# Message net: edge weight in nine contraction rows and 64 columns, scatter one-hots shared between VectorE and ScalarE

## What is computed

```python
src, dst = (edge_index[0], edge_index[1])
ew = edge_weights[:, None]
n = x.shape[0]
for l in range(edge_W.shape[0]):
    m = jnp.concatenate([x[src], x[dst], ew], axis=-1)
    m = jax.nn.relu(m @ edge_W[l] + edge_b[l])
    agg = jax.ops.segment_sum(m, dst, num_segments=n)
    x = jax.nn.relu(jnp.concatenate([x, agg], axis=-1) @ node_W[l] + node_b[l])
return x
```

## Time and profile before

| | us |
|---|---|
| median of three runs | 13607.72 |
| lowest and highest | 13596.84, 13614.53 |
| the profiled execution | 13518.01 |
| its span, first to last instruction | 13516.2 |

### The profile page before, as it was taken

The page is one execution under the profiler, slowest core; times in us unless marked ns, Lnnn a source line. Parts: engine busy times, 40 slices in busy tenths (PEclk is TensorE's granted clock), DMA queues, the critical chain, the costliest instruction groups (busy, mean ns, idle before and its releaser), DMA issues. The chain is left out here.

```text
span 13516.2 us, 456920 instructions
## 1 busy us (share of the span) xinstructions
PE 11116.6 (82%) x106911; PEld 9874.1 (73%) x106912; DVE 10913.7 (81%) x40164; ACT 5219.0 (39%) x19100; POOL 2412.2 (18%) x7659
## 2 busy tenths in 40 slices
PE   3555499899898699976664879999998779999998
PEld 3444388788787599965453339999997338999998
DVE  6555499688687388876564999999997999999998
ACT  1000122222222122235452328875453237875454
POOL 2777100000000000001110001112221001222222
PEclk9999999899898599989896999999998999999999
DMA  1111377344243011123231554432221554432222
GB/s 54 53 53 50 95 236 235 104 122 121 79 123 92 10 40 40 40 55 81 67 83 49 148 138 116 115 93 73 70 73 48 140 144 114 115 99 73 70 73 61
DMA packets 1206834, 1232.86 MB, mean 91 GB/s; under 512 B 218351, under 2 KB 1042800, under 8 KB 1206106
## 3 DMA queue, kind: packets, MB, share of 16 engines
q1 hardware_dynamic: 1180954, 1228.47, 32.9%
q0 software_dynamic: 25792, 3.35, 0.2%
HBM read 1115.06 MB, written 116.16 MB: 91 GB/s over the span
## 5 line engine op out<-in xcount | busy, mean ns | idle before, releaser
L993 DVE TENSOR_SCALAR hot<-iota_row,place 128x128 f32<-128x128 f16 (+1 forms) x9000 | 1816.7, 268 | 172.8 <-PE acc L1092 149.3
L1711 ACT ACTIVATE msgs<-G,share 128x64 f32<-128x64 f32 x6000 | 1390.0, 314 | 1351.1 <-PE G L1725 1351.1
L985 DVE TENSOR_SCALAR hotT<-idx,iota_col 128x512 bf16<-128x512 f16 x4500 | 1321.7, 351 | 603.4 <-PE G L1138 562.9
L1725 PE MATMUL G<-u_b,hotT 128*128 x12000 | 1591.7, 276 | 50.3 <-DVE hotT L1659 50.3
L1735 PE MATMUL S<-msgs,hot 128*128 128x128 f32 x12000 | 1586.3, 275 | 0.0
L1157 ACT CAST msgs<-G 128x384 bf16<-128x384 f32 x2250 | 1023.2, 479 | 1447.0 <-PE G L1138 1441.1
L1725 PEld LDWEIGHTS G<-u_b,hotT 128*128 128x128 f32 x12000 | 1467.0, 193 | 51.1 <-issue 51.1
L1735 PEld LDWEIGHTS S<-msgs,hot 128*128 128x128 f32 x12000 | 1462.3, 192 | 0.0
L1080 PE MATMUL G<-table_m,hotT 128*128 x9000 | 1311.0, 248 | 150.7 <-issue 137.6
L1110 ACT ACTIVATE msgs<-sums 128x128 f32<-128x128 f32 x2250 | 699.4, 311 | 1824.2 <-DVE sums L1102 1544.0
L1547 ACT ACTIVATE msgs<-G,msgs 128x64 f32<-128x64 f32 x6000 | 1310.8, 332 | 30.7 <-issue 21.1
(11 more groups left out here) (323 smaller groups left out, 19843.4 us busy)
## 6 DMA issues: line engine op xcount, KB each, us to landing
idx<-pos_rows SPq DMA_DIRECT2D x6375, 128.0 KB, 2.9
hotT<-hots_d SPq DMA_DIRECT2D x750, 256.0 KB
hots_d<-hotT SPq DMA_DIRECT2D x375, 256.0 KB, 3.4
key_b<-key_rows SPq DMA_DIRECT2D x62, 416.0 KB
ty_b<-type_rows SPq DMA_DIRECT2D x62, 416.0 KB
rows<-rel_rows SPq DMA_DIRECT2D x1500, 6.0 KB
ew_now<-ew_rows_d SPq DMA_DIRECT2D x1125, 3.0 KB
sorted_d<-recs,place POOLq DMA_INDIRECT x806
```

Source lines behind the costliest of these rows:

```text
L985: op = eng.tensor_scalar(hotT[:, c % deep, n], idx[:, c, r], p.col[:, first:first + 1], None, ALU.is_equal)
L993: op = eng.tensor_scalar(hot[:, c % 2, q], p.row16[:], place[:, c % 2, q:q + 1], None, ALU.is_equal)
L1711: op = eng.activation(msgs[:, c % 2, 2 + j // HEADS, j % HEADS * D:(j % HEADS + 1) * D], G[c % 2][1][:, j * D:(j + 1) * D], ACT.Copy, scal ...
L1725: mm = eng.matmul(G[c % 2][b][:, k * W:(k + 1) * W], hotT[:, c % 2, q * P:(q + 1) * P], table[:, ds(dst_at(at, q, 24 * W), W)], start=True ...
```

## The change

The edge weight's product is laid out in the other direction. `ew_rows` gets nine rows (the three parts, three times over), `ew_now` nine partitions, and `we9` holds in its nine rows each part of the weight row three times: row n is part n // 3. One matmul of 64 columns with nine contraction rows gives the sum of all nine products, and it is added to the first 64 of the chunk's 192 columns.

VectorE makes two of the four scatter one-hots (`shared_hots=2`), ScalarE the other two: first Square of (position - column) into a new tile `apart`, for the next quarter (L1114), and then Relu of 1 - `apart` into `hot` (L1126), for the present one. ScalarE signals itself (`squared`) between the two. GpSimd's copy of the places waits for `made[0]` beside the wait it had.

```diff
@@ load_sorted, SyncE
-                for i in range(EW):
-                    to = s.ew_rows[i]
+                for k in range(EW * EW):
+                    to, i = s.ew_rows[k], k % EW
@@ edge_pass, SyncE
-                        eng.dma_start(extra[0][0:EW, c], extra[1][:, ds(t * (4 * P), 4 * P)]).then_inc(idx_in[c].h, 16)
+                        eng.dma_start(extra[0][0:EW * EW, c], extra[1][:, ds(t * (4 * P), 4 * P)]).then_inc(idx_in[c].h, 16)
@@ edge_pass, GpSimd
                     ready(eng, hots, t)
+                    if shared_hots < 4:
+                        ready(eng, made[0], t)
                     eng.tensor_copy(place[:, c % 2].unsqueeze(2), s.e[:, ds(t * 4, 4), 1:2]).then_inc(placed.h, 1)
@@ edge_pass, VectorE
-                    for q in range(4):
+                    for q in range(shared_hots):
                         op = eng.tensor_scalar(hot[:, c % 2, q], p.row16[:], place[:, c % 2, q:q + 1], None,
                                                ALU.is_equal)
@@ gnn_layer, gather
-                mm = eng.matmul(env["G"][h][:, k * 3 * D:(k + 1) * 3 * D], s.ew_now[:, c, q * P:(q + 1) * P],
-                                s.we3[:, l].rearrange("p q f -> p (q f)"), start=False, stop=True)
+                mm = eng.matmul(env["G"][h][:, k * 3 * D:k * 3 * D + D], s.ew_now[:, c, q * P:(q + 1) * P],
+                                s.we9[:, l], start=False, stop=True)
@@ gnn_layer, ScalarE
+        def squares(eng, t, c, env):
+            env["reach"](eng, env["placed"], t + 1)
+            env["reach"](eng, env["made"][0], t)
+            for i in range(2):
+                op = eng.activation(apart[:, c % 2, i], p.row16[:], ACT.Square, bias=env["place"][:, c % 2, 2 + i:3 + i],
+                                    scale=-1.0)
+            op.then_inc(squared.h, 1)
+
         def scalar(eng, t, c, env):
+            if isinstance(t, int) and t == 0:
+                squares(eng, 0, 0, env)
+            if not (isinstance(t, int) and t == QUARTERS - 1):
+                squares(eng, t + 1, (c + 1) % 4, env)
+            env["reach"](eng, squared, t + 1)
+            env["reach"](eng, env["scattered"][1], t - 1)
+            for i in range(2):
+                eng.activation(env["hot"][:, c % 2, 2 + i], apart[:, c % 2, i], ACT.Relu, bias=p.ones[:, 0:1], scale=-1.0)
@@ message_net
-        fetch(p, [(s.we3[i:i + 1], we_parts[:]) for i in range(3)])
+        fetch(p, [(s.we9[n:n + 1], we_parts[:, :, n // EW]) for n in range(EW * EW)])
```

More of the change, by code:

```diff
@@ L672, in _ @@
                                   ew_rows[0:n, i, full, :]).then_inc(ld.h, 16)
-                ld.at += 48 + 96 + 32 * EW
+                ld.at += 48 + 96 + 32 * EW * EW
                 eng.wait_ge(ld.h, ld.at)
@@ L901, in src_at, with edge_pass @@
     return (words[0] >> 16).with_bounds(min_val=0, max_val=most)
-def edge_pass(p, s, rows, hot_dt, hot_parts, gather, scatter, vector, scalar, finish, extra=None, keep=None, freed=None):
+def edge_pass(p, s, rows, hot_dt, hot_parts, gather, scatter, vector, scalar, finish, extra=None, keep=None, freed=None, shared_hots=4):
     ctx = ExitStack()
@@ L934, in came @@
                 ready(eng, idx_in[c], (t - c) * (4 * ND) + 16 * ND)
-        env = dict(reach=ready, hotT=hotT, hot=hot, acc=acc, G=G, deep=deep, gathered=gathered, made=made, scattered=scattered)
+        env = dict(reach=ready, hotT=hotT, hot=hot, acc=acc, G=G, deep=deep, gathered=gathered, made=made, scattered=scattered,
+                   place=place, placed=placed)
         with p.block() as block:
@@ L1074, in gnn_layer @@
         taken = [p.fresh("taken") for _ in range(2)]
+        apart = p.sb("apart", [P, 2, 2, P], FP32, ctx)
+        squared = p.fresh("squared")
         def gather(eng, c, h, at, env):
@@ L1122, in gnn_layer @@
                   extra=(s.ew_now, s.ew_rows),
-                  keep="store" if l == 0 else "load", freed=taken)
+                  keep="store" if l == 0 else "load", freed=taken, shared_hots=2)
 def parts_pass(p, s, row, tables):
@@ L1762, in message_net @@
         we_parts = p.sb("we_parts", [1, 3, 3, D], BF16, ctx)
-        s.we3 = p.sb("we3", [P, 3, 3, D], BF16, ctx)
+        s.we9 = p.sb("we9", [P, 3, D], BF16, ctx)
         s.ew_now = p.sb("ew_now", [P, 4, 4 * P], BF16, ctx)
         ew = ins["L0_gnn_edge_W"]
-        on_vector(p, [lambda e: e.memset(bsd[:], 0.0), lambda e: e.memset(s.we3[:], 0.0),
+        on_vector(p, [lambda e: e.memset(bsd[:], 0.0), lambda e: e.memset(s.we9[:], 0.0),
                       lambda e: e.memset(s.ew_now[:], 0.0), lambda e: e.tensor_copy(s.cat[:, :, 0:D], s.x[:])])
@@ L2006, in build @@
         s.hots_d = p.dram("hots_d", [QUARTERS, P, 2 * 4 * P], BF16)
-        s.ew_rows = p.dram("ew_rows_d", [EW, CHUNKS * P], BF16)
+        s.ew_rows = p.dram("ew_rows_d", [EW * EW, CHUNKS * P], BF16)
         s.e = p.sb("e", [P, CHUNKS, REC], FP32)
```

## The result

| | before | after |
|---|---|---|
| median of four runs each, us | 13602.28 | 13541.58 |
| lowest and highest | 13587.56, 13614.53 | 13531.09, 13558.5 |
| layer 0, 1, 2: first gather to final copy, us | 842.6, 813.9, 809.4 | 809.9, 799.5, 795.7 |
| T (over 376 steps), us | 2.241, 2.165, 2.153 | 2.154, 2.126, 2.116 |
| first store of the edge-weight rows to first gather, us | 112.4 | 128.2 |

What follows compares the result with a forecast made beforehand. VectorE was taken to bound layer 0, TensorE layers 1 and 2. At 2.05 us a quarter the layers give -154 us, set-up +16, together -138 from 13608: 13470 us, range 13350 to 13640.

Steps and rivals of the forecast that it cites:

- T: Time per quarter in a layer's edge pass of the message net; forecast at 2.05 us for all three layers.
- VectorE bounds layer 0 and gets out of the way: Layer 0: two of four one-hots leave VectorE, whose time falls from 2.241 to between 1.80 and 1.85 us.
- the ring: Waits from ScalarE's messages through GpSimd's copy to ScalarE's squares and Relus: 1.96 to 2.10 us a quarter, middle 2.03.
- TensorE bounds layers 1 and 2: Layers 1 and 2: TensorE sets the mean 2.159 us a quarter and would come to 1.987 after the change.
- The slot of 64 columns: TensorE's edge-weight matmul in the gather: slot falls from 82 to about 39 ns, four saving 172 ns a quarter.
- TensorE's turn of 0.68 us is taken up: TensorE's loop repeat, every four quarters: its 0.68 us is absorbed by buffered messages where the ring is longer.
- The 0.05 for `squared`: Term of the ring: ScalarE's wait for its own squares before the Relus, between 0 and 0.11 us, taken as 0.05.
- rival D: The 64-column matmul keeps 82 ns, TensorE stays at 2.159 us, only layer 0 gains: 13593 us; chance 0.09.
- A: The forecast itself: the ring and TensorE close together, 2.05 us a quarter, 13470 us; chance 0.47.
- B: The ring is shorter than TensorE's time, TensorE alone bounds at 1.987 us a quarter: 13399 us; chance 0.24.
- Set-up: Before the layers: twelve more stores of edge-weight rows and six more small fetches add 16 us, bounds 10 and 25.
- Carrying the 89.7 us over to the median: The profiled execution is 89.7 us under the runs' median, so the 138 us gain was taken off the median 13608.

Runs made afterwards that it cites:

- block 0: Message-net blocks all numbered 0, without number loads and address arithmetic: on the changed kernel 13330.46 us, on the kernel before 13306.05 us.

## Why the prediction failed, and what of it held

**VectorE bounds layer 0 and gets out of the way: right.** It is at 90.35 of 100 us, and layer 0 gained the most, 32.7 of 60.9 us. **What is late next in layer 0: wrong.** The forecast had the ring and TensorE at 2.05; T is 2.154, for TensorE's stream needs 2.13 and SyncE's issuing of four transfers a quarter 2.13 as well. The second was a bound that the forecast never costed: it looked at the share of the DMA engines, gave the transfers nothing, and didn't ask how long SyncE takes to issue them. In the traces of before and after that share is 0.77 and 0.76, and no run shows it to bind.

**TensorE bounds layers 1 and 2: the engine was right, its part wrong.** This is the main failure. The 81 waits on "issue" of the earlier trace rows were read as the turn, and all the rest of the quarter as matmuls. With block 0 the same matmuls take 1.89 us, and before they stood at 2.16. The step of 1.93 to 1.94 us has the load of four block numbers in it (0.34 us on the sequencer), and is the same with 192 columns and with 64. The trace of before had a sign of it that I didn't look for: scatter to gather took 0.92 to 0.95 us where the eight weight loads alone take 0.87 (2799.06 to 2799.93 with block 0). The steps also differ (1.94, 2.00, 2.09) though their work is the same; the longest of these is the wait for VectorE's `sums`. "Layers 1 and 2 have a mean of 2.159, so TensorE alone would come to 1.987" took 0.172 off a time that was not made of matmuls; it gave 0.038, and that by ending a wait for VectorE.

**The slot of 64 columns: right.** The matmuls of a step take 1.73 us (one load per turn) where they took 1.89 (block 0, before): 0.16 against the 0.172 forecast. A chunk with two matmuls of 192 columns and one of 64 takes 0.19 us, 65 ns each on the mean, where three of 192 took 0.25. The Trainium skill, "TensorE: Matmul & The Clock Gate", section "Back-to-back issue gap", has about 81 ns a matmul at 128 columns in such a stream. That this would hold for 64 columns too, as rival D had it, this case's trace does not bear out.

**"TensorE's turn of 0.68 us is taken up": wrong.** The turn is TensorE's own time, and nothing makes it up while the stream binds. The gap is 0.84 with 64 columns, and 0.69 (70 waits, 48.6 us) with the sharing alone and 192. The turns of eight show its price, 0.7 us a turn, with the larger load that stands there. With block 0, where the stream doesn't bind, the step with the turn is some 0.07 longer than the others.

**ScalarE's ring, 1.96 to 2.10: right in its terms, a little long.** 1.92 measured. An ACTIVATE with a pointer took 386 to 394 ns (367 to 402 forecast) and 290 to 300 from start to start (260 to 295). The Trainium skill, "ScalarE: Activation LUTs", section "What ACT_TABLE_LOAD costs", has 280 ns + 0.833 ns a column and an overlap of about 93 ns, by which the estimate is 387 and 294 ns; the trace agrees. The 0.05 for `squared` was nothing: what the Relus wait for is a quarter old, and never belonged in the sum. But it isn't the bound in this kernel, so neither A nor B happened, and that the time lies inside the stated range, between A and D, is luck; T came out at 2.12 by a floor in TensorE's instruction stream, which no rival named.

**Set-up: right**, 15.8 us against 16. **Carrying the 89.7 us over to the median: borne out**; the sorting stage differs by 90.1 us between the two profiled executions.

In the sum: -154 forecast for the layers, -60.9 measured. Of the 93 missing, layer 0's share is 376 x (2.154 - 2.05) = 39, and layers 1 and 2 make 54 by the floor at 2.12. Of layer 0's 39 the same floor makes 26, and 13 are what is over it, with both streams near 2.13.

**Still open.** How the 0.23 us that the block numbers and the turn cost in the kernel before (0.27 less the wait of 0.04) splits is known only in part: for the load 0.2 with short matmuls (steps of 1.93 against 1.73) and less with long ones, and some 0.1 a quarter for the rest of the turn. Whether the DMA engines would let layer 0 go below 2.13 with the stores kept, what lengthens the loads of block numbers there, and why the clock held in layer 1 of the kernel with one load per turn and not in layers 0 and 2, no run here isolates.

## What to carry to other kernels

An engine that waits on "issue" need not be bound by its work: before a shorter instruction is costed as a gain, compare a loop's step with its instructions' own time from start to start, and look for register loads and turns in that engine's instruction stream, which is a bound of its own. Whether the sequencer waits can be read from the trace: where its instructions follow each other at the same distances in kernels with different matmuls, it is the bound. The same holds for the engine that issues the transfers: here SyncE needed 2.13 us for four of them and the instructions between. Here a turn of eight quarters gave 0.09 us a quarter, and the shorter matmuls and the shared one-hots together 0.04 in the same layers.

## What the hardware showed that I had not expected

- Loading block numbers into registers on TensorE's queue took 0.336 us for four words, 0.592 for eight, 1.36 for twenty: about 64 ns a word and 0.08 fixed. In layer 0, at a DMA share of 0.72, the twenty took 1.59 in the median and up to 2.14.
- TensorE's sequencer needed 8.52 us for the instructions of a turn, whether its matmuls had 192 columns or 64. The weight loads only ran closer behind it: scatter to gather 0.92 to 0.95 us with 192 columns, 1.07 with 64, 0.87 with block 0.
- A loop's turn with a load of eight block numbers left TensorE without weight loads for 0.68 to 0.84 us in the traces read above; with block 0 no such gap is seen.
- With gaps of about 1.5 us at every turn the granted clock of TensorE was 0.93 and 0.94 in stretches of two layers and 1.00 in one of the third, and a quarter took 0.19 us more at 0.94 than at 1.00.
- The handover to GpSimd took 0.2 us after ScalarE, the one back 0.04.
- Issuing four transfers a quarter took SyncE 2.13 us, 0.3 to 0.45 us for each issue and the rest for the instructions between, at a DMA share of 0.78.
